# Layer 0's edge counting: the one-hots of the low source digits move from VectorE to ScalarE

## The chip, the cores and the metric

The program runs on one core of one Trainium2 chip. The metric is the device time of one execution in microseconds; three timed runs of the kernel before are shown below, and their median is the number to predict against.

## The reference, cut to what matters

The input is a table `x` of 12500 nodes by 256 features and 200000 edges (`src`, `dst`), sorted by destination. The destinations are drawn as 12500 times the square of a uniform number, so the low destinations have by far the most edges. Three graph layers follow each other, then a gated feed-forward part:

```python
def _sage_layer(x, src, dst, inv_deg, W_self, W_neigh, b):
    agg = jax.ops.segment_sum(x[src], dst, num_segments=N_NODES)
    mean = agg * inv_deg[:, None]
    return x @ W_self + mean @ W_neigh + b
...
h = _sage_layer(features, src, dst, inv_deg, W0_self, W0_neigh, b0)
h = jax.nn.relu(h)
h = _sage_layer(h, src, dst, inv_deg, W1_self, W1_neigh, b1)
h = jax.nn.relu(h)
h = _sage_layer(h, src, dst, inv_deg, W2_self, W2_neigh, b2)
...
x = x + _L0_gnn_ref(_layernorm(x, axis=-1), src, dst, ...)
x = x + _L0_ffn_ref(_layernorm(x, axis=-1)[None], ...)[0]
```

Only the neighbour sums of layer 0, `agg`, and a count that later sums use, matter here.

## The kernel before

**Windows and gathers.** Destinations are cut into 98 windows of 128 nodes and edges into tiles of 128, four tiles to a block. For a window, TensorE multiplies, block by block, a one-hot matrix of the destinations with rows of the node table that GpSimd (POOL) fetches with indirect DMAs (L726). The rows stand in a ring of 16 tiles, and TensorE gives slots of it back as it goes (`slots_free`). VectorE makes a block's one-hots with one instruction (L1315).

**Counting.** The first 512 nodes have so many edges that they aren't gathered. For them the kernel counts, for each pair of source and destination, how many edges run between them, and multiplies the counts with node rows later. The counting lies inside layer 0's windows 2 to 33. The 512 nodes make 128 groups of 4, and each window's slot holds 4 groups. A group goes over the edge tiles that touch its nodes; for each tile the kernel makes two one-hot matrices:

- `low_hots`, 128 by 128: the low seven bits of each edge's source (L1443)
- `key_hots`, 128 by 400: the destination within the group together with the high digit of the source (L1445)

TensorE multiplies them and adds up in PSUM (`count_ps`, L846). Both matrices have rings of 4 tiles; TensorE tells through `count_used` how far it is. When the group is done, ScalarE (ACT) copies the 128 by 400 counts to a staging area (`copy_counts`, L1763). After 8 groups, which is every second window, ScalarE stores the staging area to DRAM (`store_counts`, L1770), and VectorE sums the degrees from it (`sum_degrees`, L1473).

**Order of the work around it.** Every engine runs its own instruction stream, and a stream goes on in the order in which it is written. `sub_spans` cuts the blocks of a window into 4 parts, and both TensorE (`aggregate`, L909) and VectorE (`onehots`, L1287) alternate: the first part's blocks, group 1, the second part's blocks, group 2, and so on, and one last block behind group 4. Ahead of this TensorE does the matrix products and transposes of the windows before. In window 2 alone each group is cut in halves, and `sub_spans` makes 8 parts.

ScalarE's slot (`slot_layer0`, L1887) reads: the copies and the ReLU for windows before (the last of them is `copy_zT`, L1875), then the four count copies, then two stores, and in odd slots the store of the counts. In even slots two waits stand ahead of the first count copy, because the copy overwrites the staging area:

```python
if not odd:
    act.wait_ge(counts_stored, turn * 16 + 16)
    if not isinstance(turn, int) or turn:
        act.wait_ge(degrees_summed, turn)
for k, g in enumerate(groups_of(slot)):
    copy_counts(odd * SLOT_GROUPS + k)(g)
```

The bounds of a group in tiles are known only at run time. `group_bounds` (L505) loads them from SBUF into registers (the loads are at L515): two loads per slot, and three in the slots that open a pair. TensorE and VectorE each do that for themselves. Windows 6 to 33 are a loop over pairs of windows, so there the group's number is in a register too.

Of the kernel before, what the change touches and what calls it, by code (L numbers as in the profile page):

```python
# [7 lines left out]
ALU = mybir.AluOpType  # L8
ACT = mybir.ActivationFunctionType
# [6 lines left out]
P = 128  # L16
# [22 lines left out]
def gnn_ffn_program(nc, x, src, dst, w_self, w_neigh, b_gnn, wr, br, w1, b1, w2, b2, out):  # L39
# [77 lines left out]
    with ExitStack() as ctx:  # L117
# [6 lines left out]
        def sem(name):  # L124
            return ctx.enter_context(nc.semaphore(name))
# [120 lines left out]
        flag = split[1][:].rearrange("p t d -> p (t d)").bitcast(F32)[:, 0:NT]  # L246
        rest4 = [hidT[p][:].rearrange("p k n -> p (k n)").rearrange("p (b d) -> p b d", d=D) for p in range(2)]
        zT = [hidT[p][:, 0:2 * KD, :] for p in range(2)]
        totals_ps = agg[0][:, 0:TRIALS]
        tied_ps = agg[1][0:NT, 0:1]  # L250
        earlier_ps = tp[:, 0, 0:NT]
# [43 lines left out]
        groups_ready = sem("groups_ready")  # L295
        count_hots = sem("count_hots")
        count_used = sem("count_used")
        count_ready = sem("count_ready")
        count_copied = sem("count_copied")
        counts_stored = sem("counts_stored")  # L300
# [438 lines left out]
        def _(pe):  # L739
# [97 lines left out]
            def count_group(g, bounds, halved):  # L837


                lo, end = bounds  # L840
                flags = dict(start=False, skip_group_check=True)

                def count_tile(t, stop):
                    slot = pe.snap((t + g) % COUNT_RING)
                    pe.wait_ge(count_hots, t + g + 1)
                    return mm(count_ps[:, 0:GROUP_NODES * COUNT_COLS], low_hots[:, bass.ds(slot, 1), :],  # L846
                              key_hots[:, bass.ds(slot, 1), :], stop=stop, **flags)

                def count_tiles(a, b):
                    with pe.If(a < b):  # L850
                        with pe.Fori(a, b) as t:
                            count_tile(t, False).then_inc(count_used, 1)

                def opened():
                    pe.wait_ge(count_copied, g + 2)
                    mm(count_ps[:, 0:1], zeros[:], ones_bf[:, 0:1], start=True, stop=False, skip_group_check=True)

                def closed(begin):
                    count_tiles(begin, end)
                    count_tile(end, True).then_inc(count_ready, 1)  # L860

                def whole():
                    opened()
                    closed(lo)
                if not halved:
                    return [whole]
                (_, mid), _ = sub_spans(pe, lo, end, 2)

                def first_half():
                    opened()  # L870
                    count_tiles(lo, mid)
                return [first_half, lambda: closed(mid)]
# [107 lines left out]
            def slot_layer0(w, half, p, part):  # L980
                if exists(w - 4):
                    layer_product(1, w - 4, p)
                if exists(w - 3):
                    product0(w - 3, 1 - p)
                if exists(w - 2):
                    transposes_z(w - 2, p)
                pieces = []
                slot = count_slot(w, part)
                if isinstance(w, int) and w == COUNT_AT - 2:
                    pieces = [count_ends]  # L990
                elif slot is not None:
                    halved = isinstance(w, int) and w == COUNT_AT
                    steps = [count_group(g, b, halved) for g, b in
                             zip(groups_of(slot), pe_groups(slot, w == COUNT_AT if part is None else part[2] == 0))]
                    pieces = [piece for pair in steps for piece in pair]
                    if halved:
                        pieces.pop(0)()
                rows_step = dense_step(0, w, p, part)
                dense_slot = part[0] == dense_loop(0) if part else DENSE_AT[0] <= w <= DENSE_LAST[0]
                if dense_slot:  # L1000
                    pieces = [lambda: next(rows_step, None)] * 2
                else:
                    next(rows_step, None)
                if isinstance(w, int) and w == COUNT_END:
                    dense_degrees()
                if exists(w):
                    aggregate(0, w, half, p, part, pieces)
# [94 lines left out]
        def _(dve):  # L1102
# [328 lines left out]
            def count_onehots(g, bounds, halved):  # L1431


                lo, end = bounds

                def tile_onehots(t):
                    slot = dve.snap((t + g) % COUNT_RING)
                    tile = nc.s_assert_within(
                        dve.snap(t), 0, TILES - 1,
                        skip_runtime_bounds_check_because="tiles are counted from the sorted edges, below TILES")  # L1440
                    dve.wait_ge(count_used, t + 2)
                    dve.sem_inc(dve_turn, 1)
                    v.tensor_scalar(low_hots[:, bass.ds(slot, 1), :], iota_row[:].unsqueeze(1),  # L1443
                                    src_low[:, bass.ds(tile, 1)], None, ALU.is_equal)
                    v.tensor_scalar(key_hots[:, bass.ds(slot, 1), :], iota_keys.unsqueeze(1),  # L1445
                                    group_base[:, col(g)], src_key[:, bass.ds(tile, 1)],
                                    ALU.add, ALU.is_equal).then_inc(count_hots, 1)

                def rest_onehots(begin):
                    with dve.Fori(begin, end + 1) as t:  # L1450
                        tile_onehots(t)

                def whole():
                    dve.wait_ge(count_copied, g + 1)
                    dve.sem_inc(dve_turn, 1)
                    rest_onehots(lo)
                if not halved:
                    return [whole]
                (_, mid), _ = sub_spans(dve, lo, end, 2)

                def first_half():
                    dve.wait_ge(count_copied, g + 1)
                    dve.sem_inc(dve_turn, 1)
                    with dve.If(lo < mid):
                        with dve.Fori(lo, mid) as t:
                            tile_onehots(t)
                return [first_half, lambda: rest_onehots(mid)]
# [15 lines left out]
            def slot_layer0(w, half, p, part):  # L1483
# [4 lines left out]
                if isinstance(w, int) and w == COUNT_AT - 2:  # L1488
                    pieces = [split_sources]
                elif slot is not None:  # L1490
                    degree_turn = None
                    if isinstance(w, int) and w % 2 == 0 and w > COUNT_AT:
                        degree_turn = (w - COUNT_AT) // 2 - 1
                    elif part and part[2] == 0:
                        degree_turn = part[1] + ((COUNT_LOOPED - COUNT_AT) // 2 - 1)
                    halved = isinstance(w, int) and w == COUNT_AT
                    opens = w == COUNT_AT if part is None else part[2] == 0
                    if halved:
                        steps = [count_onehots(g, b, True) for g, b in zip(groups_of(slot), dve_groups(slot, opens))]
                        pieces = [piece for pair in steps for piece in pair]  # L1500
                        pieces.pop(0)()
                    else:
                        bounds = []

                        def count_piece(k):
                            if k == 0:
                                bounds.extend(dve_groups(slot, opens))
                            count_onehots(groups_of(slot)[k], bounds[k], False)[0]()
                        pieces = [lambda k=k: count_piece(k) for k in range(SLOT_GROUPS)]
                    if degree_turn is not None:  # L1510
                        first_group = pieces[0]
                        pieces[0] = lambda: (sum_degrees(degree_turn), first_group())
# [192 lines left out]
        def _(act):  # L1705
# [52 lines left out]
            def copy_counts(j):  # L1758
# [6 lines left out]
                               "p (n k c) -> p n k c", n=GROUP_NODES, c=CHUNKS_PER_BLOCK)).then_inc(count_copied, 1)  # L1765
                return one

            def store_counts(turn):
                act.wait_ge(count_copied, turn * 8 + 10)
                act.dma_start(counts_dram[:, :, bass.ds(turn, 1), :].rearrange("c l o x -> l (c o) x"),  # L1770
                              stage.rearrange("p k n c -> p k (n c)")).then_inc(counts_stored, 16)
# [115 lines left out]
            def slot_layer0(w, half, p, part):  # L1887
# [15 lines left out]
                if slot is not None:  # L1903
                    odd = (w - COUNT_AT) % 2 if isinstance(w, int) else part[2]
                    turn = slot // 2 if isinstance(w, int) else part[1] + (COUNT_LOOPED - COUNT_AT) // 2
                    if not odd:
                        act.wait_ge(counts_stored, turn * 16 + 16)
                        if not isinstance(turn, int) or turn:
                            act.wait_ge(degrees_summed, turn)
                    for k, g in enumerate(groups_of(slot)):  # L1910
                        copy_counts(odd * SLOT_GROUPS + k)(g)
                if exists(w - 4):
                    copy_rest(1, w - 4, p, part)
# [93 lines left out]
```

## Time and profile before

| | |
|---|---|
| Timed runs | 5498.48, 5500.43, 5510.07 us; median 5500.43 us |
| Profiled execution, first to last instruction | 6674.4 us |
| TensorE, share of that span | 68% |
| VectorE | 37% |
| ScalarE | 16% |
| GpSimd (POOL) | 54% |
| Mean granted TensorE clock | 0.828 |

The profiled execution's span is 1174 us longer than the median of the timed runs. The shares are of the profiled span and average over stages that have different limits; the counting takes place from 288 to 1545 us of it. L numbers are lines of the kernel before. A "q" behind an engine's name is its sequencer, the part that handles registers, branches, waits and issue; PEld is TensorE's loading of weights.

### The profile page before, as it was taken

To read this page: it belongs to the slowest core of one execution; us is meant where nothing else is said; L and a number is where in the kernel's file an instruction comes from. 1 tells how busy PE (TensorE), PEld (TensorE's weight loads), DVE (VectorE), ACT (ScalarE), POOL (GpSimd) and SP (SyncE) were. 2 spreads that over 40 slices of the span, in tenths; PEclk is the share of its full clock that TensorE was granted. 3 is DMA by queue.
4 is the path that set the end of the run, shared out by engine and by line. 5 is a ranking of instruction groups with operands and counts; after the bars stand their busy time and mean duration, and the time that the engine had idled before them with its cause. 6 is when DMAs were issued, how large, how long until landed. Compare 5 with 4: busy or idle time off the path is not lost.

```text
span 6674.4 us, 106521 instructions
## 1 busy us (share of the span) xinstructions
PE 4538.9 (68%) x21019; PEld 2870.7 (43%) x21020; DVE 2474.3 (37%) x6444; ACT 1087.1 (16%) x2645; POOL 3592.2 (54%) x3790
## 2 busy tenths in 40 slices
PE   0465566657897775567776656664788988778884
PEld 0122223225775442244552222321566765556664
DVE  7244444443333332112222223332333344444446
ACT  6000111111112120000000000110111232223331
POOL 0544454435554665666666666656666555655551
PEclk9667777778998887788897777776889998899997
DMA  9334444445665554566665555554555654444445
GB/s 305 111 112 122 127 136 138 118 116 179 206 216 151 152 151 142 164 188 192 202 196 147 145 151 153 154 143 141 175 183 187 195 153 128 139 130 137 132 133 185
DMA packets 569508, 1057.15 MB, mean 158 GB/s; under 512 B 145479, under 2 KB 377875, under 8 KB 559827
## 3 DMA queue, kind: packets, MB, share of 16 engines
q0 software_dynamic: 241920, 743.42, 39.1%
q10 hardware_dynamic: 213078, 267.53, 11.7%
q1 hardware_dynamic: 114429, 45.18, 2.6%
q8 instruction: 43, 0.70, 0.0%
q14 instruction: 38, 0.31, 0.0%
HBM read 907.18 MB, written 148.63 MB: 158 GB/s over the span
## 4 chain that ended last, share of the span: by engine, by line
PE 31%; issue 28%; another core or an unknown queue 11%; DVEq 10%; DVE 9%; POOL 4%; ACT 3%; DMA 2%; ACTq 1%; SPq 0%; POOLq 0%
PE agg L953 10%; POOL gath L726 4%; PE y L1043 3%; PE agg L955 3%; PE hid L1033 2%; PE y L785 2%; PE lo L955 2%; PE hid L889 2%; PE lo L889 2%; PE count_ps L889 2%; DVEq L1315 2%; DVEq L1335 2%; DVEq L1450 1%; DVE onehot L1315 1%
## 5 line engine op out<-in xcount | busy, mean ns | idle before, releaser
L726 POOL DMA_INDIRECT gath<-table,idx_ring x3780 | 3590.7, 950 | 2947.8 <-issue 1280.6
L953 PE MATMUL agg<-gath,onehot 128*128 x4896 | 2055.3, 448 | 1173.0 <-issue 865.0
L953 PEld LDWEIGHTS agg<-gath,onehot 128*128 x4896 | 531.3, 109 | 1961.8 <-issue 1663.0
L955 PE MATMUL agg<-gath,onehot 128*128 x3264 | 993.6, 304 | 134.9 <-issue 129.0
L1315 DVE TENSOR_TENSOR onehot<-count_ps,dst_f 128x512 f32 x607 | 419.7, 691 | 1500.9 <-remote 706.0
L1322 DVE TENSOR_SCALAR onehot<-iota_row,window_base,dst_f 128x128 f16 x1324 | 342.4, 331 | 981.6 <-remote 344.2
L955 PE MATMUL lo<-gath,onehot 128*128 x1632 | 536.9, 329 | 36.8 <-issue 34.9
L1043 PE MATMUL y<-w_sb,hidT 128*128 128x256 f32 x1568 | 406.5, 417 | 115.0 <-ACT hidT L1947 92.8
L955 PEld LDWEIGHTS agg<-gath,onehot 128*128 x3264 | 343.2, 105 | 326.8 <-issue 240.6
L1033 PE MATMUL hid<-featT,w_gnn 128*128 128x128 f32 x3136 | 400.3, 285 | 58.1 <-issue 57.5
L1033 PEld LDWEIGHTS hid<-featT,w_gnn 128*128 128x128 f32 x3136 | 383.4, 200 | 80.1 <-issue 71.6
L1043 PEld LDWEIGHTS y<-w_sb,hidT 128*128 128x128 f32 x1568 | 320.9, 210 | 181.1 <-ACT hidT L1947 77.0
L846 PE MATMUL count_ps<-dense 128*128 x445 | 182.0, 430 | 251.0 <-issue 150.4
L1315 DVE TENSOR_TENSOR onehot<-hid,dst_f 128x512 f32 x286 | 197.7, 691 | 344.3 <-issue 179.1
L1443 DVE TENSOR_SCALAR dense<-iota_row,dense 128x128 f16 x445 | 116.8, 262 | 447.5 <-issue 368.9
L889 PE MATMUL lo<-dense 128*128 128x256 f32 (+1 forms) x784 | 247.5, 441 | 25.4 <-issue 25.4
L1726 ACT ACTIVATE featT<-tp 128x256 f32<-128x256 f32 x196 | 73.7, 376 | 1129.0 <-remote 510.3
L889 PE MATMUL count_ps<-dense 128*128 128x256 f32 (+1 forms) x784 | 236.0, 421 | 29.0 <-issue 28.9
L955 PEld LDWEIGHTS lo<-gath,onehot 128*128 x1632 | 183.3, 112 | 135.3 <-issue 76.2
L1744 ACT CAST split<-rest 128x256 bf16<-128x256 f32 x196 | 79.8, 407 | 972.0 <-DVE rest L1277 610.5
L889 PE MATMUL hid<-dense 128*128 128x256 f32 (+1 forms) x784 | 231.4, 418 | 8.9 <-issue 7.7
L785 PE MATMUL y<-w_gnn,featT 128*128 128x512 f32 x392 | 211.4, 666 | 31.4 <-ACT featT L1884 17.8
(204 smaller groups left out, 4412.0 us busy)
## 6 DMA issues: line engine op xcount, KB each, us to landing
dense<-counts_dram ACTq DMA_DIRECT2D x75, 1024.0 KB
gath<-table,idx_ring POOLq DMA_INDIRECT x3780
table<-split ACTq DMA_DIRECT2D x194, 192.0 KB
dense<-rows_f ACTq DMA_DIRECT2D x72, 512.0 KB
counts_dram<-dense ACTq DMA_DIRECT2D x16, 1600.0 KB, 8.4
rows_f<-y ACTq DMA_DIRECT2D x194, 128.0 KB
table<-gath ACTq DMA_DIRECT2D x24, 768.0 KB, 8.4
xb<-x ACTq DMA_DIRECT2D x97, 128.0 KB
```

The source lines that it names most:

```text
L726: g.indirect_dma_start(gath[:, j, 0:PARTS * D], None, table[layer][:, :], bass.IndirectOffsetOnAxis(ap=idx_ring[:, h, i:i + 1], axis=0)).t ...
L785: last = mm(product_ps(phase, p)[0:r, :], featT[p][:, k, 0:r], w, start=(k == 0), stop=(k == KD - 1))
L846: return mm(count_ps[:, 0:GROUP_NODES * COUNT_COLS], low_hots[:, bass.ds(slot, 1), :], key_hots[:, bass.ds(slot, 1), :], stop=stop, **flags)
L889: last = mm(dense_ps[layer][w], counts[p][0:r, w * P:(w + 1) * P, c], node_rows[p][0:r, c, :], start=False, stop=ends, skip_group_check=True)
L953: mm(agg[p][:, 0:2 * D], oh, tile_rows[:, :, 0:2 * D], start=False, **flags)
L955: last = mm(low, oh, tile_rows[:, :, 2 * D:2 * D + lo_cols], start=False, **flags)
L1033: last = mm(hid[:, j // 4, (j % 4) * P:(j % 4) * P + r], w1_sb[:, k, j * P:(j + 1) * P], featT[p][:, k, 0:r], start=(k == 0), stop=(k == K ...
L1043: last = mm(y0[0:r, 0:D], hidT[p][:, j, 0:r], w2_sb[:, j, :], start=(j == 0), stop=(j == KH - 1))
L1315: v.tensor_tensor(onehot[:, bass.ds(pair, GROUP), :], ids.unsqueeze(1).to_broadcast([P, GROUP, P]), dst_f[:, bass.ds(tiles, GROUP)].unsque ...
L1322: last = v.tensor_scalar(onehot[:, bass.ds(pair, GROUP), :][:, j, :], iota_row[:], window_base[:, col(w)], dst_f[:, bass.ds(tiles, GROUP)] ...
L1335: with dve.Fori(spans[-1][0], shared + 1) as b:
L1443: v.tensor_scalar(low_hots[:, bass.ds(slot, 1), :], iota_row[:].unsqueeze(1), src_low[:, bass.ds(tile, 1)], None, ALU.is_equal)
```

## The change

VectorE no longer makes `low_hots`. ScalarE makes them with two instructions per tile: `low_diff` becomes the absolute difference of the column number and the low digit, and `low_hots` is the ReLU of 1 minus that. The second waits for the first through a semaphore of ScalarE's own. The new ring `low_diff` lies in memory that is free at the time. TensorE waits for a second semaphore, `count_lows`, at each tile. ScalarE now loads the groups' bounds as well, and runs a loop over the tiles of a group ahead of each count copy. Window 2's groups aren't cut in halves any more.

```diff
                 def count_tile(t, stop):
                     slot = pe.snap((t + g) % COUNT_RING)
                     pe.wait_ge(count_hots, t + g + 1)
+                    pe.wait_ge(count_lows, t + g + 1)
...
-                    halved = isinstance(w, int) and w == COUNT_AT
+                    halved = False
...
                     dve.wait_ge(count_used, t + 2)
                     dve.sem_inc(dve_turn, 1)
-                    v.tensor_scalar(low_hots[:, bass.ds(slot, 1), :], iota_row[:].unsqueeze(1),
-                                    src_low[:, bass.ds(tile, 1)], None, ALU.is_equal)
                     v.tensor_scalar(key_hots[:, bass.ds(slot, 1), :], iota_keys.unsqueeze(1),
...
+            act_groups = group_bounds(act)
+
+            def count_low_hots(g, bounds):
+
+                lo, end = bounds
+                with act.Fori(lo, end + 1) as t:
+                    slot = act.snap((t + g) % COUNT_RING)
+                    tile = nc.s_assert_within(
+                        act.snap(t), 0, TILES - 1,
+                        skip_runtime_bounds_check_because="tiles are counted from the sorted edges, below TILES")
+                    act.wait_ge(count_used, t + 2)
+                    a.activation(low_diff[:, bass.ds(slot, 1), :], iota_row[:].unsqueeze(1), ACT.Abs,
+                                 bias=src_low[:, bass.ds(tile, 1)], scale=-1.0).then_inc(low_diffs, 1)
+                    act.wait_ge(low_diffs, t + g + 1)
+                    a.activation(low_hots[:, bass.ds(slot, 1), :], low_diff[:, bass.ds(slot, 1), :], ACT.Relu,
+                                 bias=ones[:, 0:1], scale=-1.0).then_inc(count_lows, 1)
...
                         act.wait_ge(counts_stored, turn * 16 + 16)
                         if not isinstance(turn, int) or turn:
                             act.wait_ge(degrees_summed, turn)
-                    for k, g in enumerate(groups_of(slot)):
+                    opens = w == COUNT_AT if part is None else part[2] == 0
+                    if isinstance(w, int) and opens:
+                        act.wait_ge(count_copied, 2)
+                    for k, (g, bounds) in enumerate(zip(groups_of(slot), act_groups(slot, opens))):
+                        count_low_hots(g, bounds)
                         copy_counts(odd * SLOT_GROUPS + k)(g)
```

## Rows read from the trace of the kernel before

**Rows 1.** The page: the profiled span.

```profile
span 6674.4 us, 106521 instructions
```

**Rows 2.** The chain of work behind 513 us: start, us, what.

```profile
513.91 0.69 DVEq L1450
514.60 0.70 issue
```

**Rows 3.** The counting's stretch: PE, PEld, DVE, ACT, POOL busy us; clock, DMA share, GB/s.

```profile
288.00:1545.00 1257.00, 736.72 (x2806) 342.52 (x2807) 547.77 (x1365) 150.18 (x376) 565.61 (x596) 0.71 0.43 121
```

**Rows 4.** Waits, 288 to 1545 us: engine line, waited for, us, times, longest.

```profile
POOL gath L726 <- PE lo L955: 502.7, 79, 32.7
...
PE count_ps L846 <- DVE dense L1445: 99.1, 126, 7.6
PE agg L953 <- DVE onehot L1315: 65.6, 61, 3.3
```

**Rows 5.** Window 2, TensorE's and VectorE's instructions in order of time: start, us, what.

```profile
306.32 0.51 PE L846 MATMUL count_ps<-dense 128*128 x1 [0.24 <-DVE dense L1445]
307.08 0.51 PE L846 MATMUL count_ps<-dense 128*128 x1 [0.24 <-issue]
...
316.82 0.25 DVE L1443 TENSOR_SCALAR dense<-iota_row,dense 128x128 f16 x1 [0.38 <-issue]
317.00 0.38 DVE L1445 TENSOR_SCALAR dense<-w_sb,dense 128x400 f16 x1
317.74 0.26 DVE L1443 TENSOR_SCALAR dense<-iota_row,dense 128x128 f16 x1 [0.36 <-issue]
```

**Rows 6.** Window 21 (odd slot), ScalarE, VectorE and TensorE in order of time.

```profile
1122.33 0.59 ACT L1875 COPY hidT<-tp 128x512 f32<-128x512 f32 x1
...
1122.03 0.26 DVE L1443 TENSOR_SCALAR dense<-iota_row,dense 128x128 f16 x1 [1.88 <-issue]
1122.32 0.38 DVE L1445 TENSOR_SCALAR dense<-w_sb,dense 128x400 f16 x1
1123.23 0.25 DVE L1443 TENSOR_SCALAR dense<-iota_row,dense 128x128 f16 x1 [0.53 <-issue]
...
1124.91 0.34 PE L846 MATMUL count_ps<-dense 128*128 x1 [0.57 <-issue]
1125.52 0.34 PE L846 MATMUL count_ps<-dense 128*128 x1 [0.27 <-issue]
```

**Rows 7.** TensorE's count matmuls, in all and in window 2: ns min/median/max.

```profile
L846 PE MATMUL count_ps<-dense x445: 329/492/541, 296.2 to 1543.1; 128*128 x149
...
L846 PE MATMUL count_ps<-dense x59: 340/512/541, 296.2 to 372.8; 128*128 x59
```

**Rows 8.** ScalarE's groups up to 1545 us: busy us, mean ns, idle before.

```profile
L1884 ACT ACTIVATE featT<-hid,bias 128x128 f32<-128x128 f32 x62 | 19.5, 366 | 32.8 <-remote 16.4 <-PE hid L810 15.5 <-PE tp L797 0.9
...
L1812 ACT ACT_TABLE_LOAD x1 | 1.3, 1283 | 2.5 <-POOL node_rev L699 2.5
```

**Rows 9.** Loads of bounds into registers, 1119 to 1123, then 1084 to 1091 us.

```profile
L515 DVEq FUSED_REGOPS  x4: 57/148/211, 1119.6 to 1120.9; - x4
...
L515 DVEq SEQ_ASSERT  x2: 23/28/33, 1120.4 to 1121.1; - x2
...
L515 DVEq TENSOR_LOAD <-group_pairs x3: 849/972/1057, 1086.7 to 1089.4; - x3
```

**Rows 10.** Window 20 (even slot), ScalarE's queue and TensorE in order of time.

```profile
1084.11 0.39 ACTq L1770 DMA_DIRECT2D counts_dram<-dense  x1
...
1093.68 0.92 PE L846 MATMUL count_ps<-dense 128*128 x2
1095.56 0.34 PE L846 MATMUL count_ps<-dense 128*128 x1 [0.96 <-DVE dense L1445]
```

**Rows 11.** Window 20: ScalarE's first step behind its two waits; stores' landing.

```profile
L1761 ACTq FUSED_REGOPS  x1: 43/43/43, 1093.1 to 1093.1; - x1
...
counts_dram<-dense ACTq DMA_DIRECT2D x15, 1600.0 KB, 8.4
```

More of the change, by code:

```diff
@@ L248, in gnn_ffn_program @@
         zT = [hidT[p][:, 0:2 * KD, :] for p in range(2)]
+        low_diff = hidT[1][:, 2 * KD:, :].rearrange("p k n -> p (k n)").bitcast(BF16)[:, 0:COUNT_RING * P].rearrange(
+            "p (r n) -> p r n", n=P)
         totals_ps = agg[0][:, 0:TRIALS]
@@ L297, in gnn_ffn_program @@
         count_used = sem("count_used")
+        low_diffs = sem("low_diffs")
+        count_lows = sem("count_lows")
         count_ready = sem("count_ready")
@@ L1495, in slot_layer0 @@
                         degree_turn = part[1] + ((COUNT_LOOPED - COUNT_AT) // 2 - 1)
-                    halved = isinstance(w, int) and w == COUNT_AT
+                    halved = False
                     opens = w == COUNT_AT if part is None else part[2] == 0
```

## The prediction

> **What bounds the kernel now.** I read the page first. Its span is 6674.4 us [rows 1], 1174 us more than the median of the timed runs, so the profile adds time, and I looked for where. The chain of work shows it: stretches of steps of 0.69 to 0.70 us each, one behind another, where VectorE's sequencer does nothing but handle its loop [rows 2]. I take these for the recording's own and size everything in stretches without them. So I expect a difference in microseconds to carry over to the timed runs about as it is, while the spans don't.
>
> The view by stretch gives the counting 1257 us, in which no engine is near full: TensorE 737 us, VectorE 548, POOL 566, ScalarE only 150 [rows 3]. The waits tell the order. POOL waits 502.7 us for TensorE to give ring slots back [rows 4], so the gathers don't pace this stage; TensorE does, as it goes alternately through blocks and groups. TensorE waits for VectorE in two places: 99.1 us in 126 pauses at count tiles, and 65.6 us in 61 at a block's one-hots [rows 4]. Together 164.7 us is the most that a faster VectorE can give back.
>
> The instructions in order of time show what one tile costs. In window 2 VectorE starts a low one-hot every 0.92 us (316.82, 317.74), and where VectorE is ahead TensorE takes a tile each 0.76 us (306.32, 307.08) [rows 5]. So VectorE paces the long groups. In the loop over the later windows it is otherwise: in window 21 VectorE needs 1.20 us per tile (1122.03, 1123.23), but it has finished before TensorE comes (1124.91), and TensorE takes its two tiles 0.61 us apart [rows 6]. There the pace is TensorE's sequencer, and VectorE's saving is mostly hidden.
>
> **The change part by part.**
>
> *VectorE sheds 445 low one-hots* (as many as count tiles [rows 7]), each 0.25 us long, and 0.18 to 0.29 us from its start to that of the key one-hot [rows 5, 6]. Window 2 has 59 of the tiles [rows 7], the other 124 groups 386, 3.1 each; so the block's one-hots behind a group come some 0.9 us earlier. The mean wait there is 65.6/61 = 1.08 us, so I take three quarters: 49 us. The waits at count tiles average 0.79 us, but TensorE also pauses 0.57 us there where nothing is awaited [rows 6]; what is VectorE's is 0.2 us of each, 25 us, and half of that lies in groups that ScalarE will pace: 12 us. Gain 61 us, with bounds 25 and 164.7.
>
> *ScalarE makes them in two dependent steps.* The nearest row is its activation over 128 by 128 with a bias column, out of PSUM, 366 ns [rows 8]. Between the two stands the semaphore and the second one's addresses, which the trace of ScalarE doesn't show; VectorE's addresses for the second of a pair take 0.18 us in window 2 and 0.29 in the loop [rows 5, 6]. Then the loop's step: from VectorE's second start to the next first one 0.74 and 0.91 us [rows 5, 6]. That makes 0.37 + 0.18 + 0.74 = 1.3 us per tile in window 2 and, with one semaphore step less than VectorE has, 1.5 in the loop; bounds 1.0 and 1.8. ScalarE is thus slower per tile than the engine it relieves. The Trainium skill speaks against the move too (ScalarE: Activation LUTs, Rules for kernel authors): work such as relu, max, min, add belongs on VectorE. The same page (What ACT_TABLE_LOAD costs) prices an activation with a bias column at 280 ns + 0.833 ns per element, an estimate of 387 ns here; with it the period would be 0.04 us longer and the sum some 5 us higher. The trace's 366 ns agrees.
>
> *Where ScalarE's lows stand in its stream decides.* They stand behind whatever ScalarE does first: the transposed copy, the loads of the bounds, and in even slots the two waits, which until now only held up a copy that came much later. Behind a waiting ScalarE are queued its own four groups, and TensorE waits for those; VectorE runs up to four tiles ahead and stops at the ring. Two loads on VectorE last from 1119.6 to 1121.1, 0.75 us each [rows 9], and its first low follows 0.9 us later (1122.03 [rows 6]); to the end of the second activation it is 0.9 + 0.37 + 0.29 + 0.37 = 1.9 us.
>
> - Odd slot, window 21: the loads can start with the copy at 1122.33, so the first low stands at 1122.33 + 1.5 + 1.9 = 1125.7, and the second 1.5 later at 1127.2. TensorE took them at 1124.91 and 1125.52 [rows 6]: 1.7 us late at the group's end.
> - Even slot, window 20: the counts' store is issued at 1084.11 [rows 10] and ScalarE passes its waits at 1093.1 [rows 11]. Three loads and the first pair: 1093.1 + 2.25 + 1.9 = 1097.3; the third low 3.0 later, 1100.3, where TensorE took the third tile at 1095.56 [rows 10]: 4.7 us late. This store took 9.0 us and the median is 8.4 [rows 11], so I take 4.0.
>
> The mean of the two is 2.85 us; times 28 looped slots, 80 us. Later groups of a slot have a block ahead of them, in which ScalarE makes two or three lows, and I cost them at nothing; without that cover each would cost another 1 to 2 us. For bounds: with 1.0 us per tile and loads that cost nothing, odd slots are on time and even ones 4.0 − 2 × 0.5 − 2.25 = 0.75 us late, 11 us in all. In even slots a load alone can take 0.97 us [rows 9]; with 0.5 us more for each of 2.5 loads and 1.8 us per tile it is 80 + 35 + 15 = 130 us.
>
> *Long groups.* Of window 2's 59 tiles [rows 7] the ring holds some 12 ready: 47 × (1.3 − 0.92) = 18 us. Windows 3 to 5, with groups longer than the loop's, are costed as even slots: 12 us.
>
> *TensorE's second wait.* One more sequencer step per tile; such steps take 0.04 to 0.15 us [rows 9, 11], 18 to 65 us for 445, and nothing where TensorE waits anyway. I take 10, near the low end, as the first groups and window 2 cover it.
>
> *Whole groups in window 2* save four changes between group and block at about 1 us: −4. The stores, the count copies and their DMAs stay; they move with the groups they follow.
>
> Sum: 80 + 18 + 12 + 10 − 61 − 4 = +55 us. The profiled execution would go from 6674.4 to 6729; on the timed median that is 5555. All bounds at once give −158 (11 − 164.7 − 4) and +196 (130 + 18 + 12 + 65 − 25 − 4), 5342 and 5696.
>
> **The rivals.**
>
> *VectorE's relief wins* (faster). Place: the 187 waits of TensorE for VectorE. If every low stands ready when TensorE comes, only the relief and the small terms are left: 10 − 61 − 4 = −55, 5445, and −165 at the most. It holds from the point where ScalarE has its first low within the time that TensorE's first block takes. For it speaks that ScalarE is busy only 150 of 1257 us; against it that its idle time is waiting, in the wrong places.
>
> *Nothing comes through* (no change). Without the 0.70 us steps the stage is shorter, and POOL's gathers, 596 in 566 us of work [rows 3], need at least that much of it. If they pace it then, ScalarE's lateness and VectorE's gain both fall into gather time: 5500, within 11 us. Against it: POOL's 502.7 us of waiting for TensorE.
>
> *The activation table is changed at each tile.* Up to 1545 us ScalarE loads a table once, 1283 ns [rows 8]. If the absolute value weren't in that table, 445 tiles × 2 loads × 1.28 us = 1142 us, 6640. The rows show Sqrt, ReLU and copies under one load, but not this function. By the Trainium skill (ScalarE: Activation LUTs, Table sets: the hidden batching unit) relu and abs are in every set; by that, the rival is out.
>
> **How the numbers follow.** Forecast, ScalarE behind its waits: 0.66; relief wins: 0.18; nothing comes through: 0.14; table: 0.02. The predicted time is 5555. Its own range is 5515 to 5630. As the faster rival has 0.18, the range for 8 in 10 reaches down to 5465, which leaves out its better half, and up to 5645, which leaves out slow loads joined with a slow loop. A difference of 0.2%, 11 us, is about what a measurement of this kernel can tell from no change. Faster 0.18, same 0.14, slower 0.68.
>
> **What would show it.** In the changed profile, right: ScalarE's two activations about 0.37 us each and 1.3 to 1.5 us per tile; VectorE's key one-hots 0.75 us apart in window 2; in even slots TensorE's first count tile 3 to 4 us behind its block, with ScalarE named as what it waits for, and ScalarE behind the store; fewer waits of TensorE for L1315. Wrong: TensorE's waits for ScalarE below 60 us in all; or the first lows of even slots ready before the block ends, so that VectorE's relief is all that is left.

## The result, and the profile after

The changed kernel takes 5592.56 us (median of 4 runs, 5589.39 to 5594.21) against 5500.84 us of the kernel before (4 runs beside it, 5498.48 to 5510.07): ratio 1.0167, 95% interval 1.0152 to 1.0181. It is slower by 92 us. I had forecast 5555, slower by 55, in a range of 5465 to 5645 and an own range of 5515 to 5630.

The page of the kernel after begins:

```profile
span 5590.6 us, 110383 instructions
```

Here the span lies 2 us below the run's time, not 1174 above it as in [rows 1]. The slow loop steps of [rows 2] don't show here; whether they belong to the kernel before is settled by a second recording of it, in the first experiment. Spans and waits of before are compared with that second recording from here on.

The view by stretch of the kernel after, from the first count group to the last (PE, PEld, DVE, ACT, POOL busy us; clock, DMA share, GB/s):

```profile
278.70:1346.00 1067.30, 658.24 (x2740) 326.47 (x2782) 439.69 (x914) 505.11 (x1262) 554.77 (x586) 0.79 0.49 140
```

ScalarE's 505 us stand where [rows 3] had 150, and VectorE fell from 548 to 440. No engine is near full, which points at the order of the work rather than at its amount. The waits of the kernel after, 250 to 1350 us (line, waited for, us, times, longest), answer to [rows 4]:

```profile
PE count_ps L851 <- ACT dense L1785: 157.3, 176, 4.7
...
PE agg L958 <- issue: 52.6, 104, 1.2
PE count_ps L851 <- DVE dense L1448: 44.9, 71, 1.0
...
PE lo L960 <- issue: 17.9, 26, 1.2
PE agg L958 <- DVE onehot L1320: 7.7, 14, 0.7
PE lo L960 <- DVE onehot L1320: 4.8, 5, 1.1
```

A new wait, TensorE for ScalarE, is larger than either of its two waits for VectorE was. The waits for a block's one-hots are nearly gone. ScalarE's groups up to 1350 us (busy us, mean ns, idle before) answer to [rows 8]:

```profile
L1782 ACT ACTIVATE hidT<-iota_row,dense 128x128 f16 x445 | 178.6, 401 | 250.8 <-issue 210.5 <-PE count_ps L851 36.6
L1785 ACT ACTIVATE dense<-hidT,ones x445 | 178.6, 401 | 55.7
...
L1832 ACT ACT_TABLE_LOAD x1 | 1.3, 1283 | 2.3 <-POOL node_rev L703 2.3
```

Each activation takes 401 ns, and one table load serves both functions. Of the 210.5 us of "issue" ahead of the first activation, 126 lie in 30 pauses of over 1 us (my sum over the trace), each ahead of a slot's first low; the others are steps of the loop. The chain of work at window 20, an even slot, says what such a long pause is (start us, us, what):

```profile
960.36 9.83 DMA counts_dram<-dense
970.19 0.02 issue
970.21 0.05 ACTq L519
...
972.13 0.03 issue
972.16 0.11 ACTq L1776
...
972.72 0.41 ACT hidT L1782
```

ScalarE stands behind the landing of its own store until 970.19, loads three bounds in 1.94 us (to 972.13), and starts the first low at 972.72. TensorE in order of time, window 20 and then window 21, an odd slot, with ScalarE's rows of window 21:

```profile
971.84 0.21 PE L861 MATMUL count_ps<-ones,zeros 128*128 128x1 bf16 x1
974.06 0.51 PE L851 MATMUL count_ps<-dense 128*128 x1 [2.01 <-ACT dense L1785]
975.40 0.51 PE L851 MATMUL count_ps<-dense 128*128 x1 [0.82 <-ACT dense L1785]
976.64 0.51 PE L851 MATMUL count_ps<-dense 128*128 x1 [0.73 <-ACT dense L1785]
...
996.74 0.59 ACT L1895 COPY hidT<-tp 128x512 f32<-128x512 f32 x1
998.50 0.40 ACT L1782 ACTIVATE hidT<-iota_row,dense 128x128 f16 x1 [1.17 <-issue]
999.03 0.40 ACT L1785 ACTIVATE dense<-hidT,ones  x1
999.79 0.40 ACT L1782 ACTIVATE hidT<-iota_row,dense 128x128 f16 x1 [0.36 <-issue]
```

In the second recording of before, shown below, this group's first tile starts 0.06 us behind its opening; now it is 2.2 us behind, and the tiles are as far apart as ScalarE's pairs, 1.2 to 1.3 us. In the chain over the whole counting the stores' landings, absent before, hold 13%:

```profile
by line: issue 21.2%; PE agg L958 14.7%; DMA counts_dram<-dense 13.3%; PE count_ps L851 7.7%; PE lo L960 7.1%; ACT hidT L1782 6.8%; ACTq L1782 3.2%; ACT dense L1785 2.9%; ACTq L519 2.8%; PE hid L814 2.2%; ACTq L1776 2.1%; PE y L789 1.9%; DV
```

### The profile page after: what moved, and what is told of

Same layout as the page of the kernel before. It is cut to its first block, busy times and chain, and to the rows that moved or that the text cites. A ratio compares the mean times of both kernels' runs of the same rounds, so it can differ in the third digit from the quotient of the medians.

```text
span 5590.6 us, 110383 instructions
## 1 busy us (share of the span) xinstructions
PE 4120.1 (74%) x20653; PEld 2773.7 (50%) x21020; DVE 2366.2 (42%) x5999; ACT 1442.8 (26%) x3536; POOL 3597.2 (64%) x3790
## 4 chain that ended last, share of the span: by engine, by line
PE 40%; POOL 19%; issue 17%; DMA 11%; ACT 4%; DVE 4%; ACTq 2%; DVEq 1%; POOLq 0%; SPq 0%
POOL gath L730 19%; PE agg L958 11%; DMA gath<-table,idx_ring 7%; PE y L1048 5%; PE hid L1038 4%; PE agg L960 3%; PE y L789 3%; PE count_ps L894 3%; PE lo L960 3%; DMA counts_dram<-dense 3%; PE hid L894 2%; PE hid L814 2%; PE lo L894 2%; PE count_ps L851 1%; ACT hidT L1782 1%
## 5 line engine op out<-in xcount | busy, mean ns | idle before, releaser
L958 PE MATMUL agg<-gath,onehot 128*128 x4530 | 1799.9, 428 | 793.7 <-SPq L658 682.3
L960 PE MATMUL agg<-gath,onehot 128*128 x3264 | 969.0, 297 | 155.2 <-SPq L658 105.9
L960 PE MATMUL lo<-gath,onehot 128*128 x1632 | 507.9, 311 | 45.0 <-issue 20.0
L1048 PE MATMUL y<-w_sb,hidT 128*128 128x256 f32 x1568 | 374.1, 393 | 24.2 <-ACT hidT L1971 24.2
L1038 PE MATMUL hid<-featT,w_gnn 128*128 128x128 f32 x3136 | 367.9, 276 | 0.0
L1038 PEld LDWEIGHTS hid<-featT,w_gnn 128*128 128x128 f32 x3136 | 359.9, 193 | 11.2 <-issue 0.2
L1448 DVE TENSOR_SCALAR dense<-w_sb,dense 128x400 f16 x445 | 175.3, 394 | 445.2 <-PE count_ps L851 234.7
L1729 ACT ACTIVATE featT<-tp 128x256 f32<-128x256 f32 x196 | 73.4, 375 | 1051.2 <-PE tp L776 1016.9
L1715 ACT ACTIVATE sd<-mv,eps 128x1 f32<-128x1 f32 x98 | 28.9, 294 | 978.9 <-DVE mv L1262 978.9
L1782 ACT ACTIVATE hidT<-iota_row,dense 128x128 f16 x445 | 178.6, 401 | 250.8 <-issue 210.5
L1971 ACT ACTIVATE hidT<-hid,b_sb 128x128 f32<-128x128 f32 (+1 forms) x784 | 212.5, 382 | 66.1 <-PE hid L1038 65.2
L851 PEld LDWEIGHTS count_ps<-dense 128*128 x445 | 45.4, 102 | 366.3 <-issue 363.8
```

Of the source, the lines that this page charges most:

```text
L958: mm(agg[p][:, 0:2 * D], oh, tile_rows[:, :, 0:2 * D], start=False, **flags)
L960: last = mm(low, oh, tile_rows[:, :, 2 * D:2 * D + lo_cols], start=False, **flags)
L1038: last = mm(hid[:, j // 4, (j % 4) * P:(j % 4) * P + r], w1_sb[:, k, j * P:(j + 1) * P], featT[p][:, k, 0:r], start=(k == 0), stop=(k == K ...
L1048: last = mm(y0[0:r, 0:D], hidT[p][:, j, 0:r], w2_sb[:, j, :], start=(j == 0), stop=(j == KH - 1))
L1782: a.activation(low_diff[:, bass.ds(slot, 1), :], iota_row[:].unsqueeze(1), ACT.Abs, bias=src_low[:, bass.ds(tile, 1)], scale=-1.0).then_in ...
L1971: last = a.activation(hidT[p][:, j, 0:r], hid[:, j // 4, (j % 4) * P:(j % 4) * P + r], ACT.Gelu_apprx_tanh, bias=b1_sb[:, j:j + 1])
```

## The experiments

Two readings had to be told apart: ScalarE comes late where its queue holds it (the forecast), or it is simply too slow per tile everywhere. Beside that stood the size of VectorE's relief and of TensorE's second wait. Each time stands beside the kernel before on the same chip: 5500.68 us in the first four, 5499.48 in the next four, 5500.56 in the last two. Versions of different sets are compared directly below, since these three medians agree within 1.2 us. Stage lengths and lateness are sums that I made over the trace's count matmuls, group by group.

**The kernel before, recorded once more.** No edit.

> The kernel before, unchanged, for a second profile of it. The first profile's span was 6674 us and the changed kernel's is 5591. If the steps of 0.70 us belong to that one recording, this span is near 5500 and the counting takes some 975 us, about 92 us less than the changed kernel's 1067. If they belong to the kernel before, the span is again over 6500.

One run, 5504.03 us. Its stretch, and its waits of TensorE and of POOL in the counting:

```profile
275.00:1253.00 978.00, 649.31 (x2748) 325.51 (x2795) 546.83 (x1355) 147.26 (x373) 557.62 (x588) 0.81 0.54 153
```

```profile
PE count_ps L846 <- DVE dense L1445: 81.3, 152, 1.5
PE agg L953 <- DVE onehot L1315: 56.5, 62, 1.4
PE count_ps L846 <- issue: 56.0, 158, 0.8
...
PE agg L953 <- issue: 23.9, 52, 0.9
PE lo L955 <- issue: 22.6, 20, 1.6
PE lo L955 <- DVE onehot L1315: 10.1, 9, 1.8
...
POOL gath L726 <- PE lo L955: 253.2, 65, 22.8
```

The counting takes 978 us, not the 1257 of [rows 3], with the same work in it. From the first opening to the last tile it is 977.1 us here and 1066.7 after: the 89.6 us between them are the result's 92, nearly whole. Window 20's first group, TensorE in order of time:

```profile
915.98 0.21 PE L856 MATMUL count_ps<-ones,zeros 128*128 128x1 bf16 x1
916.04 0.85 PE L846 MATMUL count_ps<-dense 128*128 x2
917.65 0.51 PE L846 MATMUL count_ps<-dense 128*128 x1 [0.75 <-DVE dense L1445]
```

It lasts 1.67 us from opening to last tile here (915.98 to 917.65), and 4.80 after.

**The first group's lows early.** The changed kernel; ScalarE loads the bounds and makes the first group's lows right behind its first copy, ahead of the other copies and of the two waits.

```diff
+                slot = count_slot(w, part)
+                if slot is not None:
...
+                    slot_bounds = act_groups(slot, opens)
+                    count_low_hots(groups_of(slot)[0], slot_bounds[0])
                 if exists(w - 4):
                     copy_product(1, w - 4, earlier(half, p, 4), p)
...
-                    for k, (g, bounds) in enumerate(zip(groups_of(slot), act_groups(slot, opens))):
-                        count_low_hots(g, bounds)
+                    for k, (g, bounds) in enumerate(zip(groups_of(slot), slot_bounds)):
+                        if k:
+                            count_low_hots(g, bounds)
```

> The changed kernel, but ScalarE loads the bounds and makes the lows of a slot's first group right behind copy_low, ahead of the other copies and of the two waits. Theory A (the place in ScalarE's stream is the cost): the first groups are on time, 28 slots gain some 2 to 3 us each, 60 to 85 us, so 5505 to 5535 us. Theory B (two dependent steps per tile are too slow wherever they stand): less than 20 us back, 5572 or more. Theory C (TensorE's second wait is the cost): nothing back, 5592.

5519.13 us, ratio 1.0034 (1.0020 to 1.0048): 73.4 us of the 92 are back, with the pair as slow as ever. The first groups of the loop are within 2 us in sum of the kernel before; the later groups still are 38.7 us longer. TensorE's waits:

```profile
PE count_ps L851 <- ACT dense L1785: 71.3, 113, 1.0
```

The longest fell from 4.7 to 1.0 us. So the place in the queue is the main cause, and a smaller one is left at the tiles. Part of what comes back is TensorE's matmul time, 642 us in the counting instead of 658, at a mean granted clock of 0.82 instead of 0.79.

**Only the two waits moved.** The changed kernel; in even slots the waits for the store and the degrees stand behind the loads of the bounds and the first group's lows.

```diff
-                    if not odd:
-                        act.wait_ge(counts_stored, turn * 16 + 16)
...
                         count_low_hots(g, bounds)
+                        if not odd and k == 0:
+                            act.wait_ge(counts_stored, turn * 16 + 16)
```

> The changed kernel, but in even slots the waits for the counts' store and the degree sums stand behind the first group's lows instead of ahead of the loads. Theory A: even slots gain what the waits hold up, 1.5 to 2.5 us in 15 slots, 22 to 37 us, so 5555 to 5570 us. Theories B and C: within 5 us of 5592.

5545.94 us, ratio 1.0089 (1.0072 to 1.0106): 46.6 us below the change. Even slots' first groups in the loop are back at the time of before, odd ones keep their lateness of 26.7 us in sum. Of the 73.4 us, the two waits in even slots are 46.6 and the copies and loads ahead of the lows the other 26.8.

**VectorE's relief alone.** The kernel before without its low one-hots (cleared once, so that all counts come out zero).

```diff
+                v.memset(low_hots, 0.0)
...
-                    v.tensor_scalar(low_hots[:, bass.ds(slot, 1), :], iota_row[:].unsqueeze(1),
-                                    src_low[:, bass.ds(tile, 1)], None, ALU.is_equal)
```

> The kernel before, but nobody makes the low one-hots: they are cleared once, so the counts come out as zero; all matmuls, copies and stores stay. It shows the most that VectorE's relief can give, with no cost on ScalarE and no second wait. Forecast by the prediction's terms: 61 us less, 5440 us, bounds 25 and 165. If VectorE's lows were hidden all along: 5490 to 5500.

5454.42 us, ratio 0.9918 (0.9902 to 0.9935): 46.3 us, where I had put 61. TensorE's waits:

```profile
PE count_ps L846 <- issue: 78.7, 202, 0.6
...
PE count_ps L846 <- DVE dense L1444: 47.6, 112, 1.1
PE agg L953 <- issue: 38.1, 82, 0.9
PE agg L953 <- DVE onehot L1315: 30.6, 39, 1.5
PE lo L955 <- issue: 23.9, 22, 1.6
...
PE lo L955 <- DVE onehot L1315: 4.0, 4, 1.2
```

Waits for VectorE shrank by 33.7 us at count tiles and by 32.0 at a block's one-hots (25.9 at L953, 6.1 at L955), 65.7 in all. The "issue" pauses, in which TensorE waits for nothing that the profile shows, grew from 23.9 to 38.1 at L953 and from 56.0 to 78.7 at count tiles. So a good part of a removed wait comes back as such a pause. The rest of the gain is TensorE's matmul time: its stretch has 632 us of it at a mean granted clock of 0.83, where the kernel before has 649 at 0.81.

```profile
274.80:1207.00 932.20, 631.61 (x2749) 320.23 (x2792) 442.82 (x914) 149.06 (x373) 555.55 (x587) 0.83 0.56 161
```

**TensorE's second wait alone.** The kernel before; VectorE signals the lows through a semaphore of their own.

```diff
                     pe.wait_ge(count_hots, t + g + 1)
+                    pe.wait_ge(count_lows, t + g + 1)
...
-                                    src_low[:, bass.ds(tile, 1)], None, ALU.is_equal)
+                                    src_low[:, bass.ds(tile, 1)], None, ALU.is_equal).then_inc(count_lows, 1)
```

> The kernel before, with VectorE's low one-hots signalling a semaphore of their own and TensorE waiting for it at each tile as well; nothing moves to ScalarE. It prices TensorE's second wait alone. By the prediction's term: 10 us, 5511, bounds 0 and 65. In the changed kernel the groups behind a slot's first one last some 27 us longer than before; if the second wait explains that, 5520 to 5530; if ScalarE's slow tiles do, 5500 to 5510.

5505.65 us (11 runs), ratio 1.0012 (1.0002 to 1.0021): 6 us, 1 to 12. By the time alone the later groups of a slot would be ScalarE's doing, as the expectation has it. The trace says otherwise: these groups last 25.1 us longer here too, with nothing moved to ScalarE. Part of it is made up at the blocks, where TensorE waits 34.2 us for one-hots instead of 66.6, with 21 more of "issue"; the counting is 11.3 us longer in all. The block waits:

```profile
PE agg L955 <- DVE onehot L1317: 29.5, 35, 1.4
...
PE lo L957 <- DVE onehot L1317: 4.7, 4, 1.8
```

**Whole groups alone.** The kernel before with `halved = False`.

> The kernel before, only without the halves in window 2. By the prediction's term 4 us less, 5497; window 2 grew by 8 us in the changed kernel, and if whole groups are what cost that, 5509.

5502.13 us (12 runs), ratio 1.0009 (1.0000 to 1.0017): a loss of 0 to 9 us where I had a gain of 4. From window 2's first opening to its last tile, with six blocks in between in both kernels, it is 71.8 us here and 68.4 before.

**One activation in place of two.** The changed kernel without the ReLU step: the absolute difference itself stands in the low one-hots.

```diff
-                    act.wait_ge(low_diffs, t + g + 1)
-                    a.activation(low_hots[:, bass.ds(slot, 1), :], low_diff[:, bass.ds(slot, 1), :], ACT.Relu,
-                                 bias=ones[:, 0:1], scale=-1.0).then_inc(count_lows, 1)
```

> The changed kernel without the second activation: the absolute difference goes straight into the low one-hots' ring, so the counts come out wrong; every wait of the others stays. ScalarE's time per tile should fall from 1.29 us to 0.75 or 0.85. If the dependent pair is a large part of the loss, the spacing inside first groups (27 us in the loop) and window 2's growth go away and the later groups gain: 5540 to 5555. If the place in the stream is nearly all of it, 5565 to 5580.

5531.55 us, ratio 1.0067 (1.0049 to 1.0084): 61 us less than the change, yet still slower than before. By the trace 35 us of that lie in the loop's first groups (each starts one step earlier) and 13 in window 2. But even slots' first tiles remain 24.9 us late in sum: half the work per tile doesn't cure a late start.

**Early first group and a single wait.** As the second experiment; TensorE waits for ScalarE alone, and ScalarE's second activation waits for VectorE's keys.

```diff
-                    pe.wait_ge(count_hots, t + g + 1)
                     pe.wait_ge(count_lows, t + g + 1)
...
                     act.wait_ge(low_diffs, t + g + 1)
+                    act.wait_ge(count_hots, t + g + 1)
```

> The version with early lows, but TensorE waits for ScalarE's signal alone, and ScalarE's second activation waits for VectorE's key one-hots of the tile. Against 5519 us for early lows: if TensorE's second wait is what keeps that version behind the kernel before, 5495 to 5505; if ScalarE's pace does, 5515 to 5525, as its loop gets one more step.

5494.37 us (11 runs), ratio 0.9989 (0.9980 to 0.9998): 24.8 us below the early first group alone. The later groups, 38.7 us longer than before there, are 23.1 longer here.

**The single wait by itself.** The changed kernel with that last edit only.

> The changed kernel with TensorE waiting for ScalarE alone, whose second activation waits for VectorE's keys; everything else as in the change. If TensorE's second wait is a step of its own price in all 445 tiles, this gives back the 25 us by which the two edits together beat the early first group alone: 5565 to 5570 us. If the late lows of the first groups cover it there, as I forecast, it gives back less than 15 us: 5578 to 5590.

5570.87 us, ratio 1.0127 (1.0112 to 1.0143): 21.7 us below the change. By the trace 18.7 us of it lie in the loop's second to fourth groups and only 2 in the first ones, which are late anyway. The second wait costs about 0.05 us per tile (21.7 / 445), and nearly all of it in groups where ScalarE is on time.

**The two steps taken apart.** Early first group and single wait; besides, the absolute difference of tile t+1 is issued ahead of the ReLU of tile t, without a wait for TensorE.

```diff
-                    act.wait_ge(count_used, t + 2)
...
+                diff(lo)
+                with act.If(lo < end):
+                    with act.Fori(lo, end) as t:
+                        diff(t + 1)
+                        hot(t)
+                hot(end)
```

> The changed kernel with the first group's lows made right behind ScalarE's first copy, TensorE waiting for ScalarE alone (ScalarE's second activation waits for VectorE's keys), and in addition the two activations taken apart: the absolute difference of tile t+1 is issued ahead of the ReLU of tile t, and it no longer waits for TensorE, since only ScalarE uses its ring. If what is left of the loss is the dependence inside ScalarE's pair (0.18 us or more of each 1.3 us per tile, as it was seen with one activation alone: window 2's spacing 8 us shorter), the counting gets 15 to 25 us shorter than with the two edits alone, 5470 to 5480 us, faster than both kernels. If ScalarE's sequencer paces its loop (two sets of addresses per step), nothing is gained and the time is 5490 to 5505.

5467.47 us (5 runs), ratio 0.9934 (0.9921 to 0.9948): faster than both kernels, 26.9 us below the version without it, and 13 above VectorE's relief alone. ScalarE in order of time in a long group, and the counting's stretch:

```profile
360.03 0.40 ACT L1788 ACTIVATE dense<-hidT,ones  x1
360.52 0.40 ACT L1781 ACTIVATE hidT<-iota_row,dense 128x128 f16 x1
360.86 0.40 ACT L1788 ACTIVATE dense<-hidT,ones  x1
...
364.74 0.40 ACT L1788 ACTIVATE dense<-hidT,ones  x1 [2.17 <-DVE dense L1447]
```

```profile
279.00:1218.00 939.00, 638.08 (x2792) 319.67 (x2789) 440.60 (x914) 477.92 (x1258) 554.15 (x584) 0.84 0.56 159
```

A tile costs ScalarE 0.83 us (360.03 to 360.86), the two activations nearly back to back, and what it waits for at 364.74 is VectorE's keys. Over the counting its ReLU waits 132.7 us for these keys, and they in turn 129.8 us for tiles that TensorE gives back. The later groups are 14.9 us longer than before. Two things changed at once in this kernel, the order of the steps and the dropped wait for TensorE; their shares were not told apart.

## Why the prediction was right, and where its terms were off

**Direction and mechanism held.** "Where ScalarE's lows stand in its stream decides" is shown by the second and third experiments: with nothing moved but the bounds' loads and the first group's lows, 73.4 of 92 us come back. The chain names the store, as forecast for even slots.

**First groups: right.** Forecast 1.7 us per odd slot, 4.0 per even, 80 in all. The trace gives 1.9 and 3.2 (26.2 and 44.8 us over 14 slots each), 71 in all. The sign "first count tile 3 to 4 us behind its block" did not come true as written: in even slots of the loop the first tile starts 2.4 us behind the opening in the mean, and the rest of the lateness is in the tiles' spacing. The experiment's 73.4 also holds part of windows 3 to 5, which I had at 12 and the trace has at 13. Three loads took 1.94 us instead of 2.25, and ScalarE's period was mostly 1.19 to 1.35 us instead of 1.5, which both make it less; the store took 9.5 us in the median instead of 8.4, which makes it more (9.6 in the second recording of before, so it did not become slower).

**VectorE's relief: too large.** The step that failed is the mean wait taken at its face. "I take three quarters: 49 us" of the block waits did come true as a change of waits: in the kernel after they went from 66.6 us (56.5 and 10.1) to 12.5 (7.7 and 4.8), 54 less. But TensorE's "issue" pauses at the same blocks rose from 46.5 to 70.5, so 30 of them were left as time. By itself the relief is 46.3 us, where I had 61. I had not asked how long TensorE would still pause there without waiting for another engine.

**Second wait: too small.** Forecast 10, "as the first groups and window 2 cover it". They do, and the later groups don't: 21.7 and 24.8 us in two places. In the kernel before it is 6, although the later groups lengthen by 25.1 us there: part of what it costs at the tiles TensorE no longer waits for at the blocks. So its price depends on which wait it replaces.

**Later groups: the term that I set to nothing.** "Later groups of a slot have a block ahead of them … I cost them at nothing." In the loop they are 27.3 us longer after the change (2.5 in the first tile, 24.8 in the spacing of the others). The block covers the first tile, as I wrote, and not the pace of the rest. 18.7 of the 27.3 are the second wait by the changed kernel without it, and the kernel before with it has 25.1 in the same groups; so most of the term is the second wait. With the first group early these groups are 38.7 us above before, 23.1 with the single wait as well, and 14.9 with the pair also taken apart: the single wait takes 15.6 off, the pair with its wait for TensorE 8.2.

**Window 2.** Forecast +18 for the pace and −4 for whole groups, 14 together. From the window's first opening to its last tile the trace has 68.4 us before and 77.1 after, 8.7 more, and 71.8 with whole groups alone. So whole groups cost 3.5 by that trace and saved nothing, and 5.2 are left for the rest of the change there. VectorE's relief alone takes 6.4 off the same stretch, so for ScalarE's pace I estimate 12 where I had 18. In the kernel after, ScalarE's low one-hots there (start us, us, what):

```profile
319.74 0.40 ACT L1782 ACTIVATE hidT<-iota_row,dense 128x128 f16 x1 [0.19 <-issue]
320.26 0.40 ACT L1785 ACTIVATE dense<-hidT,ones  x1
...
320.85 0.40 ACT L1782 ACTIVATE hidT<-iota_row,dense 128x128 f16 x1 [0.19 <-issue]
```

The period is 1.11 us here and 1.20 in the window's median, not 1.3, although an activation takes 401 ns and not 366: from the second start to the next first one it is 0.59 us here (320.26 to 320.85), where I had taken VectorE's 0.74. VectorE's keys were to come 0.75 us apart; in the same stretch they come 1.03 apart, each behind a tile that TensorE gives back, and TensorE waits for ScalarE there.

**The sum.** From the change down, each step the difference of two measured versions: 73.4 for the late first groups, 24.8 for the second wait, 26.9 for the pair with its wait for TensorE, 13.1 not taken apart further (whole groups among them), and −46.3 for the relief: 92. Another order of the steps would give other shares; the single wait is 21.7 by itself. The changed kernel's own trace adds up too: 71.0 in first groups, 27.3 in later ones, 13.0 in windows 3 to 5 and 8.7 in window 2 are 120; the blocks, with 54 us less of waiting and 24 more of "issue", take off 30; that leaves 90, against the 89.6 measured. My terms in the same order: 92 (80 + 12), 10, 14 (18 − 4) for the two of the pair, and −61. Too much for the first, too little for the next ones; they offset each other in part, and 37 us are left between 55 and 92.

**The rivals.** "VectorE's relief wins" needs every low ready when TensorE comes. A version near that state took 5467 us against the 5445 that I gave it, but only with three further edits, and TensorE still waits 100.0 us there for ScalarE's signal, which then stands for VectorE's keys too. The rule of the Trainium skill that such work belongs on VectorE (ScalarE: Activation LUTs, Rules for kernel authors) agrees with the change as it was made, 5592.56 us, and not with that version. Of the loss, 73.4 us are the place in the queue and not the engine. "Nothing comes through" is out: POOL still waits 347.5 us for TensorE in the kernel after, so the gathers don't pace the stage. The table's change at each tile is out by the one table load that stands above; the Trainium skill (ScalarE: Activation LUTs, Table sets: the hidden batching unit) has relu and abs in every set, and the trace agrees.

```profile
POOL gath L730 <- PE lo L960: 347.5, 72, 26.9
```

**The odd recording.** I took the 0.70 us steps for the recording's own and worked without them. The second recording confirms that they are not the kernel's: VectorE's loop instructions at L1450 have the same medians in both, and last 0.71 to 1.36 us at the longest in the first and 0.14 in the second. TensorE's and SyncE's sequencers were slowed in the first recording too. Whether the profiler did it or that one execution isn't shown, and the profiled span that I forecast, 6729 us, fell with it. What I didn't do was to scale the waits that I took from it: POOL's 502.7 us in [rows 4] are 253.2 without them, and the 99.1 and 65.6 us are 81.3 and 56.5.

## What to carry to other kernels

Work that moves to an idle engine inherits that engine's queue: look at what stands ahead of it there, waits for stores above all, since a wait that held up only a late copy now holds up the first product. Place the moved work ahead of such waits, let the consumer wait for one producer that has itself waited for the other, and issue the first half of a dependent pair one turn early; here these three turned a loss of 92 us into a gain of 33. And count a removed wait only down to what the waiting engine would pause there anyway: here 24 of the 54 us that blocks no longer waited came back as "issue".

## What the runs showed of the hardware

- A recorded execution can be slower than the timed runs: 6674.4 us of span for a kernel of 5500, with stretches of VectorE's loop handling at 0.70 us a step, and 5502.2 us for the same kernel recorded again. What made it slow isn't shown.
- An activation over 128 by 128 with a bias column took 401 ns from SBUF and 366 from PSUM [rows 8]; the two differ in number type and destination as well. Two that don't depend on each other follow at 0.83 us for the two, while a dependent pair with its loop took 1.11 to 1.36 us.
- Loading three bounds into registers, with the register work behind each load, took ScalarE 1.94 us in the chain of window 20. Of that the load instruction itself is 283 ns in the median of all 79; VectorE's load of the same values is 911 ns in the second recording of before.
- In the counting, TensorE's mean granted clock was 0.79 in the changed kernel and 0.84 in the version with the pair taken apart, and its work, the same in both, took 658 and 638 us. The runs don't tell whether the clock is only a consequence of fewer pauses.
